# Both feed-forward products by one level of Strassen's scheme, the first over all rows before the second

## The reference

```python
x = _ln(src) * (1.0 + scale) + shift
...
ctx = ctx.transpose(0, 2, 1, 3).reshape(B, S, D)
x = x + (ctx @ Wo + bo)
h = _ln(x) * g2 + beta2
ff = _gelu2(h @ W1 + b1) @ W2 + b2
return x + ff
```

## Time and profile before

| | us |
|---|---|
| three runs, median (lowest to highest) | 2565.6 (2565.1 to 2567.06) |
| the profiled execution | 2566.05 |
| its span, first to last instruction | 2564.3 |
| feed-forward half, first matmul to last | 1094.8 to 2559.0 |
| TensorE busy / VectorE / ScalarE / GpSimd | 97% / 51% / 38% / 38% |

### The profile page before, as it was taken

The page is one execution under the profiler, slowest core; times in us unless marked ns, Lnnn a source line. Parts: engine busy times, 40 slices in busy tenths (PEclk is TensorE's granted clock), DMA queues, the critical chain, the costliest instruction groups (busy, mean ns, idle before and its releaser), DMA issues.

```text
span 2564.3 us, 46326 instructions
## 1 busy us (share of the span) xinstructions
PE 2496.1 (97%) x16402; PEld 2084.7 (81%) x16402; DVE 1309.4 (51%) x2515; ACT 968.7 (38%) x3183; POOL 972.2 (38%) x830
## 2 busy tenths in 40 slices
PE   4999999999999999799999999999999999999999
PEld 3888888888888888678888888888888888888887
DVE  4777777777777776554233323323333333332332
ACT  2666666666666666632211121121111112112111
POOL 3777777777777777521011011101101101110100
PEclk8999999999999999899999999999999999999999
DMA  7444444444444443231000000000000000000000
GB/s 232 126 134 134 135 134 136 134 137 134 135 135 135 135 140 107 68 115 58 1 33 33 33 0 33 33 0 33 33 4 29 33 33 0 33 33 0 33 17 17
DMA packets 205879, 187.33 MB, mean 73 GB/s; under 512 B 20224, under 2 KB 159616, under 8 KB 205696
## 3 DMA queue, kind: packets, MB, share of 16 engines
q1 hardware_dynamic: 205696, 184.99, 23.0%
HBM read 151.14 MB, written 33.82 MB: 72 GB/s over the span
## 4 chain that ended last, share of the span: by engine, by line
PE 56%; POOL 0%; DVE 0%; DMA 0%; issue 0%; SPq 0%; ACT 0%; DVEq 0%
PE psY L1026 9%; PE psY L1028 9%; PE psY L1027 9%; PE psH L1028 9%; PE psH L1027 9%; PE psH L1026 9%; PE turn L207 1%; DMA b_bc<-in_b 0%; POOL r L941 0%; DVE r L1001 0%; DVE wo_hi L986 0%; DVE w_lo L991 0%; POOL r L180 0%; DVE w_lo L994 0%; DVE wo_hi L984 0%
## 5 line engine op out<-in xcount | busy, mean ns | idle before, releaser
L959 ACT ACTIVATE gf<-psH,b_c 128x512 f32<-128x512 f32 x256 | 176.8, 691 | 1181.6 <-PE psH L1028 1181.6
L984 DVE CAST wo_hi<-gf 128x512 fp32r<-128x512 f32 x256 | 116.3, 454 | 878.6 <-ACT gf L959 878.6
L1026 PE MATMUL psY<-w_hi,wo_hi 128*128 128x512 f32 x1024 | 410.4, 401 | 1.1 <-DVE wo_hi L986 1.1
L1026 PE MATMUL psH<-hT_hi,w_hi 128*128 128x512 f32 x1024 | 405.6, 396 | 5.9 <-DVE w_lo L991 5.9
L1028 PE MATMUL psH<-hT_hi,w_lo 128*128 128x512 f32 x1024 | 406.1, 397 | 0.0
L1027 PE MATMUL psH<-hT_lo,w_hi 128*128 128x512 f32 x1024 | 405.5, 396 | 0.0
L1028 PE MATMUL psY<-w_hi,wo_hi 128*128 128x512 f32 x1024 | 405.0, 396 | 0.0
L1027 PE MATMUL psY<-w_lo,wo_hi 128*128 128x512 f32 x1024 | 404.4, 395 | 0.0
L612 ACT ACTIVATE s<-s,nmx 128x128 f32<-128x128 f32 x1024 | 398.4, 394 | 7.9 <-issue 5.0
L560 POOL TENSOR_TENSOR s<-s,rinv 128x512 f32<-128x512 f32 x256 | 266.7, 1042 | 239.3 <-DVE rinv L681 238.9
L553 POOL TENSOR_TENSOR bias<-bias,mneg 128x512 f32<-128x512 f32 x256 | 335.3, 1332 | 10.8 <-DVE mneg L686 10.8
(11 more groups left out here) (134 smaller groups left out, 4594.1 us busy)
## 6 DMA issues: line engine op xcount, KB each, us to landing
bias<-in_bias SPq DMA_DIRECT2D x128, 512.0 KB, 5.3
adab<-ada_rows SPq DMA_DIRECT2D x64, 512.0 KB, 5.3
xin<-in_x SPq DMA_DIRECT2D x32, 512.0 KB, 4.2
resid<-rout SPq DMA_DIRECT2D x64, 256.0 KB, 2.1
r<-resid SPq DMA_DIRECT2D x16, 1024.0 KB, 5.6
out<-r SPq DMA_DIRECT2D x64, 256.0 KB, 2.1
raw_o<-in_W SPq DMA_DIRECT2D x32, 256.0 KB, 3.0
w_ada<-in_W_ada SPq DMA_DIRECT2D x1, 2048.0 KB, 10.6
```

The costliest lines, as they stand in the source:

```text
L959: act.activation(gf[:, j % 2, :], psH[j % 2][:, :], ACT.Gelu_apprx_sigmoid, bias=b1_c[:, j:j + 1]).then_inc(gelu_done, 1)
L984: dve.tensor_copy(gT[0][:, j % 2, :], gf[:, j % 2, :]).then_inc(g_hi, 1)
L1026: pe.matmul(out_ap, sh, mh, start=start, stop=False)
```

## The change

A product of two matrices cut into quarters needs eight products of quarters; Strassen's scheme (here in Winograd's form) makes it from seven, of which four take sums of quarters as factors, and the results are sums of the seven. The change does this for both products, with quarters named by `FACTOR` (index of the stationary and of the moving factor among 3 raw and 4 combined ones that count). It also takes the two products apart: all 16 groups go through the first, whose gated columns are stored in a DRAM tensor `gated` (0.5 MB per unit), then all go through the second.

- A unit is 2 x 128 hidden columns by 512 rows; there are 8 units in each of the 16 groups, in either half. Each unit has 7 products of 6 matmuls with 256 moving columns: 42 where there were 48 such widths before (24 matmuls of 512).
- First half, TensorE in the order 1, 6, 7, 5, 2, 4, 3; products 1 and 5 share a bank. ScalarE copies products 1 and 5 out (`copy_p1`, `copy_p5`). VectorE makes the sums with a bank as one input (`u2_u3`, `c11`, `c21`, `c12`), GpSimd two sums over product 5 (`c22_u4`), ScalarE gates the unit (`gate`) one unit later, SP stores it. The normalized rows of the next group need combined factors too: in units 3 and 5 ScalarE copies the transposes, GpSimd makes four sums (`sums`), ScalarE rounds the raw and then the combined factors (`high`), VectorE makes their low parts a unit later (`low`). Rows `r` have one buffer now, and the bias adds for the group after next stand at unit 6.
- Second half: SP loads a unit's gated columns, GpSimd makes four sums, ScalarE rounds, VectorE makes the low parts, two units ahead of TensorE, in two buffers `gs`. The seven results add up over the 8 units of a group in seven banks. At a group's end VectorE and ScalarE take them out (`drain`), and GpSimd makes the eight closing sums (`finish`), one to two per unit of the next group.
- Weights need the same combined factors: those of `W1` in the first group (only unit 0 is loaded ahead), those of `W2`, into the same place, in the last group of the first half.
- After attention's last steps the end of the first half is followed by `before_down`, which prepares the first two units of the second; the last group's closing sums stand alone at the end of the kernel.

```diff
+A_TYPE = ((4, 0, ALU.add, 3), (5, 4, ALU.subtract, 1), (6, 1, ALU.subtract, 0), (7, 2, ALU.subtract, 5))
+B_TYPE = ((4, 0, ALU.subtract, 1), (5, 3, ALU.subtract, 4), (6, 3, ALU.subtract, 0), (7, 2, ALU.subtract, 5))
+FACTOR = {1: (0, 0), 2: (1, 1), 3: (6, 2), 4: (2, 6), 5: (3, 3), 6: (4, 4), 7: (5, 5)}
+RAW, COMBINED = slice(0, 3), slice(3, 7)
+def combine(eng, t, kind, done, count, ready):
+    for m, (to, a, op, b) in enumerate(kind):
+        if m in (1, 3):
+            at_least(eng, done, count * 3 + (1 if m == 1 else 2))
+        ins = eng.tensor_tensor(t[:, to, :], t[:, a, :], t[:, b, :], op)
+        if m < 3:
+            ins.then_inc(done, 1)
+        else:
+            ins.then_inc(ready, 1)
...
+    def sums(self, pool, n, e):
+        at_least(pool, self.xt_copied, n * 4 + (e * 2 + 2))
+        combine(pool, self.hTf, B_TYPE, self.t_part, n * 2 + e, self.t_sums)
+    def high(self, act, n, u, e, piece):
+        at_least(act, self.xt_copied, n * 4 + (e * 2 + 2))
+        if piece:
+            at_least(act, self.t_sums, n * 2 + (e + 1))
+        ops = (RAW, COMBINED)[piece]
+        act.activation(self.T[u][:, 0, ops, e, :], self.hTf[:, ops.start + 1:ops.stop + 1, :], ACT.Copy).then_inc(self.t_hi, 1)
+    def low(self, dve, n, u, e, piece):
+        at_least(dve, self.t_hi, (n * 2 + e) * 2 + (piece + 1))
+        ops = (RAW, COMBINED)[piece]
+        dve.tensor_tensor(self.T[u][:, 1, ops, e, :], self.hTf[:, ops.start + 1:ops.stop + 1, :],
+                          self.T[u][:, 0, ops, e, :].bitcast(F32), ALU.subtract).then_inc(self.t_ready, 1)
...
+        psU = {1: up_bank[0], 5: up_bank[0], 6: up_bank[1], 7: up_bank[2], 2: up_bank[3], 4: up_bank[4], 3: up_bank[5]}
+        flat = [t[:, :, :].rearrange("p c k -> p (c k)") for t in psX]
+        acc = {1: flat[0], 2: flat[1]} | {i: up_bank[b][:, :] for i, b in ((4, 1), (6, 2), (7, 0), (5, 3), (3, 4))}
...
+        UP_ORDER = (1, 6, 7, 5, 2, 4, 3)
+        ACC_ORDER = (1, 2, 4, 6, 7, 5, 3)
...
+            def c22_u4(k, s):
+                at_least(pool, u3_ready, k + 1)
+                at_least(pool, p5_copied, k + 1)
+                pool.tensor_tensor(gu[:, s, 3, :], gu[:, s, 2, :], p5c[:, :], ALU.add).then_inc(c22_ready, 1)
+                pool.tensor_tensor(gu[:, s, 0, :], gu[:, s, 0, :], p5c[:, :], ALU.add).then_inc(u4_ready, 1)
+            def up(n, j, u, first):
+                if not (first and j == 0):
+                    c22_u4(n * J + (j - 1), (j - 1) % 4)
+                if first and j + 2 < J:
+                    weights.sums(pool, j + 2)
+                if fixed(n) and n == LAST and j:
+                    weights.sums(pool, J + j - 1)
...
+                        norm.add_bo(pool, n + 1, b)
+                if has(n, 1):
+                    if j == first:
+                        norm.root(pool, n + 1)
+                    if j in sums_at(first):
+                        norm.sums(pool, n + 1, sums_at(first).index(j))
+                if has(n, 2) and j == 6 + first:
+                    for b in range(NB):
+                        norm.add_bo(pool, n + 2, b)
...
+            def finish(n, u, m):
+                r11, r12, r21, r22 = quarters(u)
+                to, by = ((r11, c1), (r11, e2), (u2d, e5), (r12, u2d), (r21, u3d), (r21, e4), (e5, u3d), (r22, e5))[m]
+                at_least(pool, drained, n * 5 + 5)
+                at_least(pool, copied, n * 2 + 2)
+                at_least(pool, y_part, n * 8 + m)
+                pool.tensor_tensor(to, to, by, ALU.add).then_inc(y_part, 1)
+            def down(n, j, u, first):
+                if not first:
+                    for m in ((0,), (1,), (2, 3), (4,), (5,), (6,), (7,), ())[j]:
+                        finish(n - 1, 1 - u, m)
+                if has(n, 1) or j + 2 < J:
+                    sums(n * J + (j + 2), (j + 2) % 4)
...
+            def copy_p1(k):
+                at_least(act, up_done, after(k, 1))
+                at_least(act, c11_ready, k)
+                act.activation(p1c[:, :], psU[1][:, 0:H], ACT.Copy).then_inc(p1_copied, 1)
...
+            def up(n, j, u, first):
+                k = n * J + j
+                copy_p1(k)
+                if not (first and j == 0):
+                    gate(k - 1, (j - 1) % J, (j - 1) % 4)
+                copy_p5(k)
+                if has(n, 1):
+                    if j in sums_at(first):
+                        for half in range(2):
+                            norm.copy(act, n + 1, sums_at(first).index(j), half)
+                if first and j + 2 < J:
+                    for piece in range(2):
+                        weights.high(act, j + 2, piece)
+                if fixed(n) and n == LAST and j:
+                    at_least(act, up_done, k * 7)
+                    for piece in range(2):
+                        weights.high(act, J + j - 1, piece)
+                if has(n, 1) and j in highs_at(first):
+                    e = highs_at(first).index(j)
+                    if e == 0:
+                        at_least(act, up_done, n * (J * 7))
+                        if first:
+                            act.wait_ge(weights.w_ready, 2 * J)
+                    for piece in range(2):
+                        norm.high(act, n + 1, 1 - u, e, piece)
...
+            def high(k, s):
+                at_least(act, g_in[s], (k - s) // 4 * DMA + DMA)
+                at_least(act, acc_done, (k - 1) * 7)
+                act.activation(gs[s % 2][:, 0, RAW, :], gbuf[s][:, 1:4, :], ACT.Copy).then_inc(s_hi, 1)
+                at_least(act, s_sums, k + 1)
+                act.activation(gs[s % 2][:, 0, COMBINED, :], gbuf[s][:, 4:8, :], ACT.Copy).then_inc(s_hi, 1)
...
+            def u2_u3(k, s):
+                at_least(dve, g_out[s], (k - s) // 4 * DMA)
+                at_least(dve, up_done, after(k, 6))
+                at_least(dve, p1_copied, k + 1)
+                dve.tensor_tensor(gu[:, s, 0, :], psU[6][:, 0:H], p1c[:, :], ALU.add).then_inc(u2_ready, 1)
+                at_least(dve, up_done, after(k, 7))
+                at_least(dve, u2_ready, k + 1)
+                dve.tensor_tensor(gu[:, s, 2, :], psU[7][:, 0:H], gu[:, s, 0, :], ALU.add).then_inc(u3_ready, 1)
+            def c11(k, s):
+                at_least(dve, up_done, after(k, 2))
+                dve.tensor_tensor(gu[:, s, 1, :], psU[2][:, 0:H], p1c[:, :], ALU.add).then_inc(c11_ready, 1)
+            def c21(k, s):
+                at_least(dve, up_done, after(k, 4))
+                at_least(dve, c22_ready, k + 1)
+                dve.tensor_tensor(gu[:, s, 2, :], psU[4][:, 0:H], gu[:, s, 2, :], ALU.add).then_inc(c21_ready, 1)
+            def c12(k, s):
+                at_least(dve, up_done, after(k, 3))
+                at_least(dve, u4_ready, k + 1)
+                dve.tensor_tensor(gu[:, s, 0, :], psU[3][:, 0:H], gu[:, s, 0, :], ALU.add).then_inc(c12_ready, 1)
...
+            def low(k, s):
+                for piece, ops in enumerate((RAW, COMBINED)):
+                    at_least(dve, s_hi, 2 * k + (piece + 1))
+                    dve.tensor_tensor(gs[s % 2][:, 1, ops, :], gbuf[s][:, ops.start + 1:ops.stop + 1, :],
+                                      gs[s % 2][:, 0, ops, :].bitcast(F32), ALU.subtract).then_inc(s_ready, 1)
...
+            def product(i, j, u):
+                a, b = FACTOR[i]
+                for e in range(2):
+                    last = three(psU[i][:, 0:H], [wc[:, j, h, a, e * P:(e + 1) * P] for h in range(2)],
+                                 [T[u][:, h, b, e, :] for h in range(2)], e == 0, e == 1)
+                last.then_inc(up_done, 1)
+            def up(n, j, u, first):
+                k = n * J + j
+                freed = {1: (p5_copied, k), 6: (u2_ready, k), 7: (u3_ready, k), 5: (p1_copied, k + 1),
+                         2: (c11_ready, k), 4: (c21_ready, k), 3: (c12_ready, k)}
+                for i in UP_ORDER:
+                    if i in (1, 6):
+                        if first:
+                            pe.wait_ge(weights.w_ready, 2 * j + (1 if i == 1 else 2))
+                        if j == 0:
+                            at_least(pe, norm.t_ready, n * 4 + (3 if i == 1 else 4))
+                    at_least(pe, *freed[i])
+                    if i == 2 and has(n, 1) and j in turns_at(first):
+                        for half in range(2):
+                            norm.transpose(pe, n + 1, turns_at(first).index(j), half)
+                    product(i, j, u)
...
+                for i in ACC_ORDER:
+                    if i == 1:
+                        at_least(pe, s_ready, 2 * k + 1)
+                    if i == 6:
+                        at_least(pe, s_ready, 2 * k + 2)
...
+                    a, b = FACTOR[i]
+                    for half in range(2):
+                        last = three(acc[i][:, half * H:(half + 1) * H], [gs[j % 2][:, h, a, half * P:(half + 1) * P] for h in range(2)],
```

(3 more changed lines are left out.)

595 lines of the change are left out of this document (382 added, 213 removed).

## The result

| | before | changed kernel |
|---|---|---|
| median of the runs shown | 2565.35 us (2564.82 to 2567.06, 4 runs) | 2740.62 us (2739.25 to 2742.39, 4 runs) |
| profiled execution | 2566.05, span 2564.3 | 2741.64, span 2739.8 |
| first feed-forward matmul starts | 1094.80 | 1109.27 |
| both products, first matmul to last | interleaved, 1464.2 | first half 834.3, second half 773.0, with 7.9 between |

The ratio is 1.0685 (95% interval 1.0672 to 1.0698): the change costs 175 us. The forecast was 2673 with a range of 2590 to 2760. The sign and the range hold; the forecast is 68.6 us too low against the profiled execution.

What follows compares the result with a forecast made beforehand. The prediction took TensorE's matmul stream to bound the kernel after 1094.8 us (97% busy). Sum: 2566 - 172 + 112 + 100 + 27 + 8 + 7 + 10 + 15 = 2673 us, range 2590 to 2760.

Steps and rivals of the forecast that it cites:

- Matrix work, -172: TensorE, both halves: seven products for eight, 10752 matmuls of 256 columns at 0.1175 us, a gain of 172 us.
- the seventh saved isn't saved: Rival on TensorE's matmuls: small ones run at 0.127 us or more, 102 us more, 2775 us; chance 0.04.
- First half, steady groups, +112: TensorE waits 2.5 us before product 5 twice a group, units 7 and 0 lose about 3.2: 112 us (60 to 170).
- Second half, +100: VectorE's lows and GpSimd's adds exclude one another, 5.78 us a unit against TensorE's 4.94: 100 us.
- loads, stores and the bank drains lie beside it: Second half: loads, stores and emptying of banks were taken to run alongside, with no time of their own in the sum.
- has no closing adds and stays hidden: First group of the second half: without closing adds, no wait counted; the 0.84 us a unit applies to 15 groups only.
- Start and first group, +27: First half's start: later sums in attention's tail (+3), weight units and collisions cost 27 us (15 to 45).
- Last group of the first half, +8: Second weight set there: seven units at +0.9 us and a late fetch, 8 us.
- Clock, +15 in the first half, none in the second: TensorE's clock falls after a quarter of the first half's 28 waits of 2.5 us: 15 us.
- the clock falls at every wait: Rival, first half: low clock after all 28 waits costs 64 us instead of 15, 2722 us; chance 0.15.
- No exclusion: Rival, second half: VectorE and GpSimd interleave without loss or seldom meet, TensorE's pace holds, 2573 us; chance 0.12.
- The gain survives: Rival, first half: sums are ready in time, so ScalarE's wait doesn't reach product 5, 2546 us; chance 0.08.

Runs made afterwards that it cites:

- late_round: Changed kernel with ScalarE's rounding of the first half's four sums one unit later, behind copy and gate, and VectorE's low part behind `c11`: 2737.3 us.
- sums_first: Changed kernel; in each second-half group's first unit GpSimd forms the next unit's sums ahead of its first closing add: 2713.7 us.
- all: Changed kernel with first-half order edits, second-half sums on VectorE with one bank emptied ahead of them, and attention-tail feed-forward sums behind the last probabilities: 2601.9 us.
- all_paced: `all` with each GpSimd closing add waiting until VectorE has formed that unit's sums: 2514.6 us.
- all_paced_root: `all_paced` with GpSimd's power of the normalisation and VectorE's four normalisations one unit later: 2510.2 us.
- second_half: Changed kernel with second-half sums on VectorE instead of GpSimd and, in a group's last unit, only one bank emptied ahead of the sums: 2701.0 us.
- short_low: Changed kernel with VectorE's low part of the plain factors cut to 8 columns from unit 2 of the second half on (stale values): 2663.4 us.

## Why the prediction was right in sign and range, and 69 us too low

| term | forecast | measured |
|---|---|---|
| start and first group of the first half, from 1094.80 | 70.5 | 88.4 |
| groups 2 to 15 of the first half | 704 (50.3 each) | 716.4 (51.2 each) |
| last group of the first half | 47.5 | 44.0 |
| between the halves | 7 | 7.9 |
| first group of the second half | 39.5 | 51.9 |
| groups 2 to 15 of the second half | 646 (46.2 each) | 676.3 (48.3 each) |
| its last group | 46.2 | 44.6 |
| last matmul to the end | 15.3 | 15.3 |

(Measured from one group's first matmul to the next's, the last group of a half to its last matmul. The forecast column spreads the sum's own terms over groups: 42 x 8 slots of 0.1175, transposes, stands, and the clock's 15 us on the first half.)

- **Matrix work, -172: right, a little small in price.** Undisturbed units, by the first matmuls of one unit and the next: a unit 3 of the first half, then units 1 and 2 of the second:

```profile
1509.29 0.29 PE L1358 MATMUL up<-T,wc 128*128 128x256 f32 x1
...
1514.33 0.29 PE L1358 MATMUL up<-T,wc 128*128 128x256 f32 x1
...
2299.47 0.28 PE L1358 MATMUL turn<-wc,gs 128*128 128x256 f32 x1
...
2309.44 0.28 PE L1358 MATMUL turn<-wc,gs 128*128 128x256 f32 x1
```

  42 slots in 5.04 us are 0.1200, 84 in 9.97 are 0.1187 (the mean of such units in the middle groups is 4.97 us, 0.1183); forecast 0.1175. Over the 5376 matmuls of the first half that is 13 us, and 4 in the second. The rival "the seventh saved isn't saved" (0.127) is refuted.
- **First half, steady groups, +112: right in place, cause and size, but not a single cause.** Groups 2 to 15 took 716.4 where the sum has 704. The dearer matmuls are 12 us of it. What is left for stands and low clock together is 127 us, as forecast, but split otherwise: about 21 of low clock instead of 15, and so some 106 of stands instead of 112. 2.50 us were lost at units 4 and 6, as forecast. Here luck has a part: the sum's own terms, a copy done at 9.4 and a product wanted at 7.05, give 2.35 and not the 2.5 that it counts. In the unit shown product 5 started 9.70 us after unit 3's start (9.4 forecast: the four sums took 2.92 instead of 2.56), and it was wanted about 0.15 later than forecast as well, since the slots are longer. `late_round` shows that removing the named cause alone gains nothing: two more queues stand behind the same sums.
- **Second half, +100: the mechanism right, one term missing.** Cycle 5.75 against 5.78, though its parts were each a little off: alone, four sums take 2.94 (I had 2.56) and a closing add 1.30 (1.23), while the low parts cost GpSimd 1.60, not their full 1.99. These errors cancel, so that the cycle came out within 0.03 is partly luck. The step that failed is "loads, stores and the bank drains lie beside it". The emptying of the banks does not take GpSimd's time, but it holds its queue for 2.2 us a group, and the time of an engine that bounds isn't given back. 14 x 2.1 = 30 us; `sums_first` took 27 of it out.
- **First group of the second half: not in the sum, 12 us.** This is a second step that failed. I wrote that it "has no closing adds and stays hidden". GpSimd's queue there has the last weight unit's sums and the two instructions on the bias rows in front of the sums of unit 1, and both wait for loads. TensorE stands twice at unit 1: 4.3 us before its first product, for a low part that VectorE takes behind the last weight unit's, and 1.8 us before product 6, for the low part of the sums:

```profile
1954.52 3.65 POOL L161 TENSOR_TENSOR raw<-raw 128x256 f32<-128x256 f32 x4 [2.56 <-DMA raw<-in_W]
...
1959.97 1.73 POOL L1127 TENSOR_TENSOR bo_bc<-bo_bc,part_p 128x512 f32<-128x512 f32 x1 [1.80 <-DMA part_p<-in_b]
...
1963.07 2.92 POOL L161 TENSOR_TENSOR gbuf<-gbuf 128x256 f32<-128x256 f32 x4
```

- **Start and first group, +27: too small by 18.** The tail of attention was put at +3. GpSimd's two sets of sums stand before the last probabilities, by way of ScalarE's exponentials, and TensorE stood 7.06 us there:

```profile
1081.68 2.88 POOL L161 TENSOR_TENSOR hTf<-hTf 128x256 f32<-128x256 f32 x4
1084.66 1.06 ACT L244 ACTIVATE T<-hTf 128x1024 fp32r<-128x1024 f32 x1 [5.79 <-POOL hTf L161]
...
1088.63 1.11 PE L854 MATMUL psS<-ident,s 128*128 128x128 f32 x4 [7.06 <-POOL s L617]
```

  In `all`, with those sums behind the probabilities, the first product starts at 1099.02 instead of 1109.27, and in `all_paced` and `all_paced_root`, which change nothing there, at 1101.4 and 1101.2. The first group's 73.9 us are also more than forecast. Its longest stand is 7.7 us, at its end before the first product of group 2: the low part that TensorE waits for is in VectorE's queue behind statistics of rows, which waited 8.9 us for GpSimd's bias adds. No run took this group apart.
- **Last group of the first half, +8:** 4.5 us over 39.5. **Between the halves, +7:** 7.9. **End, +10:** as forecast.
- **Clock, +15 in the first half, none in the second: wrong in the second, without effect there.** Behind the 3.42-us stand at a group's start, which ended at 2389.69, the granted clock is 0.50 (1.2 of 2.4 GHz) for nearly six microseconds:

```profile
2391.00:2392.00 1.00, 1.00 (x7) 1.00 (x7) 1.00 (x3) 0.41 (x1) 0.00 (x0) 0.50 0.88 360
...
2396.00:2398.00 2.00, 2.00 (x19) 2.00 (x18) 0.00 (x0) 0.47 (x1) 1.96 (x3) 1.00 0.75 180
```

  The first four products there take 1.28 to 1.45 us instead of 0.71. `sums_first` has the same low clock and a group of 46.5, GpSimd's 8 x 5.8: TensorE's lost cycles lay beside GpSimd's. In `second_half` they count: a group of 45.5 is TensorE's own 39.8, a stand of 3.6 and about 2 at low clock. In the first half the 2.34-us stand shown above ended at full clock (granted clock 1.00 from 1516 to 1520), so the rival "the clock falls at every wait" does not hold; behind others it did fall, by 0.4 us on average at product 5 of unit 4. All slots at the low level together exceed the normal ones by 29 us in the first half (7 of them in its slow first group) and by 35 in the second.
- **The rivals of the other side.** "No exclusion" is refuted by `short_low`. "The gain survives" needed the sums off the path; `all_paced` shows what it takes.

## What to carry to other kernels

When a change lowers the work of the engine that bounds and gives its neighbours more, price the neighbours' queues in order, not by their sums: all three edits of order here cost no arithmetic and were worth 92 us, and moving sums and pacing eight adds was worth 124 more. When a queue becomes the bound, each wait inside it counts in full, even one on an engine that is idle most of the time. And after relieving an engine ask what it will now do all at once: here one added wait gave back 84 us.

## What the runs showed of the hardware

- VectorE and GpSimd, both with two inputs in SBUF, lengthen one another in both directions: GpSimd's four adds from 2.94 to 3.97 and 4.54 us under one and two subtractions; VectorE's four adds from 1.55 to 5.78 under a run of GpSimd's. A VectorE subtraction of 8 columns takes 0.16 us alone and 0.70 beside GpSimd's adds (`short_low`). VectorE's additions from the product banks keep their 0.68 to 0.69 us: in the changed kernel one takes 0.69 from 2341.28 on, while GpSimd's last sum of the set runs until 2341.90.
- A 128x256 add costs GpSimd 0.73 us and a 128x512 add 1.30: half the width is 56% of the price. VectorE takes 0.39 each for four in a row.
- The price of a 256-column matmul depends a little on the stage: 0.1200 in the first half, 0.1183 in the second. Which operand or neighbour makes the difference was not tried.
